# A chunked recurrent layer on one NeuronCore: the state's product as three passes of split parts

## The reference

```python
xn = layernorm(x)
proj = einsum('bld,pd->blp', xn, in_proj_w)      # gate, hbc (x, B, C) and dt
xBC = silu(causal_conv4(hbc))                    # x: 64 heads x 64; B, C: 8 groups x 128
dt = softplus(dt + dt_bias); dA = exp(-exp(A_log) * dt)
# per token t, head h:  state = state * dA + (dt * x) outer B;   y = state @ C
y = y + x * D
yn = y * rsqrt(mean_over_group(y * y) + eps) * norm_weight * silu(gate)
s = einsum('bli,di->bld', yn, out_proj_w)
out = x + s * silu(xn @ W.T + bias + lora)
```

## Time and profile before

| | |
|---|---|
| three runs | 1748.84, 1750.83, 1754.08 us, median 1750.83 |
| the profiled execution | 1753.88 us, of which the span is 1752.1 |
| mean granted TensorE clock | 0.991 of full speed |
| PE / PEld busy | 97% / 78% of the span |
| DVE / POOL / ACT busy | 81% / 68% / 63% |
| DMA | 304.78 MB, mean 174 GB/s |
| chain that ended last, by engine | PE 80%, DMA 5%, DVE 5%, SP's queue 4%, ACT 2%, POOL 2% |

### The profile page before, as it was taken

One profiled execution on the slowest core, in us unless ns is written; L12 is line 12 of the kernel. 1 busy time (PEld: TensorE's weight loads), 2 busy tenths in 40 slices (PEclk: granted clock), 3 DMA queues, 4 the chain that ended last, 5 costly groups with the idle time before them and its releaser, 6 DMA issues.

```text
span 1752.1 us, 31626 instructions
## 1 busy us (share of the span) xinstructions
PE 1697.6 (97%) x10792; PEld 1368.7 (78%) x10792; DVE 1420.8 (81%) x1840; ACT 1098.3 (63%) x2843; POOL 1190.4 (68%) x1255
## 2 busy tenths in 40 slices
PE   7988999999999999999998999999999999999986
PEld 5777888888888888888876888888888888888865
DVE  7868888887978888887876978888887878888885
ACT  4557576665757576665656667575666657576653
POOL 5428677675857767675786858678575857767564
PEclk9999999999999999999999999999999999999998
DMA  8545555555555555555787655565555565555555
GB/s 267 157 134 171 171 176 153 169 173 173 166 177 159 164 169 164 179 173 157 232 227 230 184 174 161 166 180 154 169 174 174 154 184 160 165 166 177 159 166 151
DMA packets 322416, 304.78 MB, mean 174 GB/s; under 512 B 88272, under 2 KB 255568, under 8 KB 322256
## 3 DMA queue, kind: packets, MB, share of 16 engines
q1 hardware_dynamic: 321216, 302.60, 58.0%
q10 hardware_dynamic: 1040, 0.16, 0.1%
HBM read 246.57 MB, written 56.10 MB: 173 GB/s over the span
## 4 chain that ended last, share of the span: by engine, by line
PE 80%; DMA 5%; DVE 5%; SPq 4%; issue 3%; ACT 2%; POOL 2%; ACTq 0%; POOLq 0%; DVEq 0%
PE ps_conv L1381 9%; PE ps_conv L1384 9%; PE ps_y L1544 7%; PE ps_conv L1387 6%; PE ps_out L1381 6%; PE ps_gate L1381 6%; PE ps_s L1565 6%; PE ps_out L1384 6%; PE ps_gate L1384 6%; PE ps_y L1549 5%; PE ps_out L1387 4%; PE ps_gate L1387 4%; DMA turned_d<-squares 3%; PE ps_conv L1388 2%; PE ps_g L1373 2%
## 5 line engine op out<-in xcount | busy, mean ns | idle before, releaser
L930 DVE SCALAR_TENSOR_TENSOR xc<-ps_conv,convw_sb,xc 128x511 f32<-128x511 f32 (+2 forms) x576 | 430.4, 747 | 96.7 <-ACT xc L694 83.1
L1288 POOL TENSOR_TENSOR cpre<-cpre,xc 128x1024 f32<-128x1024 f32 x112 | 268.5, 2397 | 52.8 <-ACT xc L700 29.9
L826 ACT ACTIVATE dtx<-x_tok,prefix_dt 128x64 f32<-128x64 f32 x1024 | 258.1, 339 | 72.1 <-DMA b_tok<-turned_d 72.0
L1321 POOL TENSOR_TENSOR square<-square 128x256 f32<-128x256 f32 x128 | 93.8, 733 | 305.6 <-ACT square L838 305.6
L1070 DVE TENSOR_TENSOR_SCAN decay<-decay,turned_x 128x512 f32<-128x512 f32 x250 | 290.4, 1203 | 9.2 <-DMA decay<-decays_d 9.0
L1381 PE MATMUL ps_conv<-xn_hi,wconv_hi 128*128 128x512 f32 x768 | 245.4, 441 | 0.0
L1384 PE MATMUL ps_conv<-xn_hi,wconv_lo 128*128 128x512 f32 x768 | 206.4, 390 | 0.0
L1381 PEld LDWEIGHTS ps_conv<-xn_hi,wconv_hi 128*128 128x128 f32 x768 | 144.4, 188 | 68.2 <-issue 43.6
L1544 PE MATMUL ps_y<-decay,dtx 128*64 128x128 f32 x1984 | 191.6, 280 | 2.7 <-ACT ps_y L808 2.7
L854 ACT ACTIVATE ynt_hi<-ps_y 128x512 fp32r<-128x512 f32 x126 | 75.2, 597 | 178.2 <-DVE ps_y L1128 175.1
L1549 PE MATMUL ps_y<-cpre,state 128*64 128x128 f32 x1760 | 172.1, 274 | 0.0
(11 more groups left out here) (236 smaller groups left out, 3783.0 us busy)
## 6 DMA issues: line engine op xcount, KB each, us to landing
decay<-decays_d SPq DMA_DIRECT2D x125, 512.0 KB, 5.1
cpre<-rows_d SPq DMA_DIRECT2D x112, 512.0 KB, 4.1
turned_d<-squares SPq DMA_DIRECT2D x512, 80.0 KB, 2.7
stage<-w_in_t SPq DMA_DIRECT2D x32, 1024.0 KB, 6.3
x_tok<-turned_d SPq DMA_DIRECT2D x128, 256.0 KB, 3.0
stage<-w_out_t SPq DMA_DIRECT2D x16, 1024.0 KB, 6.3
stage<-w_in_t SPq DMA_DIRECT2D x32, 256.0 KB, 3.9
b_tok<-turned_d SPq DMA_DIRECT2D x128, 64.0 KB, 2.9
```

Of the source, the lines that this page charges most:

```text
L826: scaled = e.activation(dtx[i % 2][:, h * HD:(h + 1) * HD].rearrange("p (a i) -> p a i", i=SQ), head_of(x_tok[i % 2], h), ACT.Copy, scale= ...
L930: e.scalar_tensor_tensor(acc[:, d:], ps[:, 0:BLK - d], convw_sb[:, tile, TAPS - 1 - d:TAPS - d], acc[:, d:], ALU.mult, ALU.add).then_inc(S ...
L1288: e.tensor_tensor(cpre[k % 2][:, :, :], cpre[k % 2][:, :, :], xc[i // CPB % 2][:, XT + 1, block_cols(i % NCH)].unsqueeze(1).to_broadcast([ ...
```

## The change

The product of L1565 is no longer one native fp32 matmul. `b_tok` and `xw` are each split, as the weights are: ACT makes `b_hi` (128 x 128) and `xw_hi` (128 x 512) by copies to fp32r, at the head of its step before the `dtx` scalings, and POOL makes `b_lo` and `xw_lo` by subtraction at the very head of its step, before `left_of_state`. PE runs the three passes b_hi by xw_hi, b_lo by xw_hi, b_hi by xw_lo. The four new tiles have one buffer each. In the diff below, the first `e.activation` lines are ACT's, `split_state` and `scale_x` are POOL's, and the last hunk is PE's. `scale_x` waits for `xw_lo` of the step before, on its own queue.

```diff
+        xw_hi = sb("xw_hi", [P, GC], F32R)
+        xw_lo = sb("xw_lo", [P, GC], F32R)
+        b_hi = sb("b_hi", [P, NS], F32R)
+        b_lo = sb("b_lo", [P, NS], F32R)
...
                 if 0 <= m < N and conv_late(m) is not None:
                     conv(conv_late(m))
+                if 0 <= m < N and m % NCH < NCH - 1:
+                    w.wait_ge(landed_tok[m % 2], 32 * (m // 2 + 1))
+                    w.wait_ge(S["mm_u"], inner(m) - 1)
+                    e.activation(b_hi[:, :], b_tok[m % 2][:, :], ACT.Copy).then_inc(S["b_hi"], 1)
+                    w.wait_ge(S["xw"], inner(m))
+                    e.activation(xw_hi[:, :], xw[:, :], ACT.Copy).then_inc(S["xw_hi"], 1)
...
+            def split_state(m):
+                w.wait_ge(S["b_hi"], inner(m))
+                w.wait_ge(S["mm_u"], inner(m) - 1)
+                e.tensor_tensor(b_lo[:, :], b_tok[m % 2][:, :], b_hi[:, :].bitcast(F32), ALU.subtract).then_inc(S["b_lo"], 1)
+                w.wait_ge(S["xw_hi"], inner(m))
+                e.tensor_tensor(xw_lo[:, :], xw[:, :], xw_hi[:, :].bitcast(F32), ALU.subtract).then_inc(S["xw_lo"], 1)
...
             def scale_x(i):
-                w.wait_ge(S["mm_u"], inner(i) - 1)
+                w.wait_ge(S["xw_lo"], inner(i) - 1)
...
                 m, u = i - 1, i - DRAIN
                 f = finished(i)
+                if 0 <= m < N and m % NCH < NCH - 1:
+                    split_state(m)
                 if i < N and i % NCH > 0:
                     left_of_state(i)
...
-                    w.wait_ge(landed_tok[m % 2], 32 * (m // 2 + 1))
-                    w.wait_ge(S["xw"], inner(m))
+                    w.wait_ge(S["b_hi"], inner(m))
+                    w.wait_ge(S["xw_hi"], inner(m))
                     w.wait_ge(S["state"], inner(m - 1) if m > 0 else 0)
-                    e.matmul(ps_s[:, :], b_tok[m % 2][:, :], xw[:, :], start=True, stop=True).then_inc(S["mm_u"], 1)
+                    passes(ps_s[:, :], (lambda t: b_hi[:, :], lambda t: b_lo[:, :]),
+                           (lambda t: xw_hi[:, :], lambda t: xw_lo[:, :]), 1,
+                           lambda: w.wait_ge(S["b_lo"], inner(m)), lambda: w.wait_ge(S["xw_lo"], inner(m)), S["mm_u"])
```

More of the change, by code:

```diff
@@ L244, in build @@
             landed_rows0 landed_rows1 st_rows10 st_rows11 st_rows00 st_rows01
-            turned st_turned landed_tok0 landed_tok1 dtx scan last xw mm_g M skip cpre mm_gate sgate mm_in mm_u
+            turned st_turned landed_tok0 landed_tok1 dtx scan last xw b_hi xw_hi b_lo xw_lo mm_g M skip cpre mm_gate sgate mm_in mm_u
             seed state sdec square sum1 sum2 mm_ssq var2 rstd2 yg hi2 lo2 mm_out osum
```

## The result

| | before | after |
|---|---|---|
| median of 7 runs each, us | 1752.9 (1748.8 to 1754.1) | 1758.2 (1756.7 to 1760.2) |
| the profiled execution, us | 1753.88, span 1752.1 | 1757.41, span 1755.4 |
| ratio after / before | | 1.0035, 95% interval 1.0023 to 1.0046 |

The change makes the kernel 0.35% slower. 1744 and a faster kernel were forecast (the change from the profiled execution of before was to be -6.8 us; it is +3.5, and +5.3 between the medians).

The account below looks back on a forecast made before the run. PE was taken to bound 14 of 16 groups. Terms -17.5 (PE), +4.2 (third pass), +5.0 (last group), +1.5 (batch's turn) gave -6.8 us: 1747.1 for the profiled execution, 1744.0 for a median; range 1736 to 1760.

Parts of the forecast that it names:

- The product's price on PE: On PE, native product 0.86 us against 0.68 for three passes: 0.18 saved per product, 17.5 us over 97.
- Rival 3: On PE, three passes into one bank cost as much as the native product, no saving: 1761 us; chance 0.06.
- The four durations: Added operations on POOL and ACT: xw_lo 1.30 us, b_lo 0.46, xw_hi 0.62, b_hi 0.30.
- Third pass at position 1: PE wants xw_lo at 432.07, it ends at 432.1, PE starts at 432.3: a stall of 0.2 to 0.3 us.
- At position 2: PE's third pass: xw_lo at 446.15, wanted at 446.22, just in time; a stall of 0.05 to 0.1 us.
- Position 4: PE's third pass: xw_lo at 470.6, wanted at 471.8, a slack of 1.0 us and so no stall.
- I cost it at nothing: Work behind POOL's split_state: cpre, rstd2 and out_sum come late, out_sum some 1.6 us, but DVE's slack covers it: 0 us.
- The copies "in an idle time of 2.09 before dtx": On ACT at position 1, b_hi and xw_hi run to 430.8 in 2.09 us of idle time, so dtx isn't late.
- First batch's last group and what follows: POOL delays the batch's turn by 1.5 us, bounds 0 and 5; PE's stalls there fall into its later waits.
- Last group: split_state comes ahead of cpre on POOL's chain, two to four times: 5.0 us slower, bounds 0 and 9.
- The second: Rival: PE waits for xw_lo in a POOL, ACT, POOL, PE loop, about 0.5 us per stalled product: 1764 us; chance 0.17.
- The first: Rival: POOL 0.5 us later at positions 2 to 5, PE stalls 0.8 to 1.0 us per group: 1752 us; chance 0.25.

Follow-up runs that it names:

- experiment 1: The change without POOL's two subtractions, PE using the hi parts in all three passes: 1735.7 us, ratio 0.9912 to the kernel before.
- Experiment 8: The change cut to one pass of rounded values, xw written as fp32r by POOL, no low parts, not the same computation: 1689.9 us, ratio 0.9651.
- Experiments 7: The change with ACT's copies b_hi and xw_hi moved ahead of the late tile's tap: 1746.2 us, ratio 0.9963 to the kernel before.
- 10: The change with POOL's cpre ahead of the subtractions at position 3 alone: 1751.7 us, ratio 1.0002 to the kernel before.
- experiment 12: The change with ACT's copies ahead of the tap and the native product wherever fin_multiply and fin_add precede POOL's subtractions: 1737.1 us, ratio 0.9911.
- 2: The change with the native product back in each batch's last group and for step 64's product: 1750.7 us, ratio 1.0002 to the kernel before.
- 9: The change with ACT's copies ahead of the late tap and the native product in groups 7 and 15: 1738.2 us, ratio 0.9932.
- experiment 5: The change with PE reading only hi parts and not waiting for low parts, which POOL still makes: 1757.3 us, ratio 1.0031 to the kernel before.

## Why the prediction was wrong, by its steps

Forecast against measured, both from the profiled executions (12 ordinary groups: 12 x 0.96 = 11.5 of the 97 products' gain less the stalls; group 0: steps 2 to 7). With the first product of both batches left out the forecast should have counted 14 x 7 - 2 = 96 products, a slip of 0.2 us.

| | forecast | measured |
|---|---|---|
| 12 ordinary groups | -11.5 | -4.1 |
| group 0 | -1.0 | +0.6 |
| group 7 | +1.5 | +2.8 |
| group 8 | -0.8 | +2.4 |
| group 15 | +5.0 | +2.7 |
| ahead of group 0's step 2, behind group 15 | 0 | -1.2 |
| sum | -6.8 | +3.3 (the span's) |

- **The product's price on PE: right.** 0.86 less 0.68 was to be 0.18; it is 0.19 (11.43 to 11.24), and experiment 1 gives it seven times per group. Rival 3 is out. Experiment 8 is the check of 0.2275 per pass.
- **The four durations: right** (1.28, 0.46, 0.63, 0.31 against 1.30, 0.46, 0.62, 0.30).
- **Third pass at position 1: right** (0.23). **At position 2 the size came right by luck** (0.10). The rows were those of group 3, where xw ended 1.56 us ahead of PE's sum of squares; in nine of the twelve ordinary groups of before it was 3.0 to 3.2. After, it is 1.41 in all but one.
- **Position 4: the failed step.** It read "a slack of 1.0" from ACT's timeline of before, with b_hi 2.7 ahead of PE's product (468.5 and 471.23). After, b_hi is 1.4 ahead (468.17 and 469.57), and the slack is gone. Measured from PE's sum of squares at position 3 or 4, out_sum came 2.2 us later than before, the taps behind it 1.7, and ACT's silu and b_hi 1.3. Position 6, which had "more", stalls by 0.16 in the same way.
- **What made it fail is the next step, "I cost it at nothing".** It had cpre 2 us late at positions 2 and 4 and out_sum 1.6. Against PE's step cpre is 3.8 and 3.2 late there in the median, and out_sum 2.8 and 3.1. It closed with DVE's mean slack and the 4 to 6 us until PE wants the output. The path that counts doesn't end at the output: it goes rstd2, out_sum, early taps, ACT's silu, b_hi, b_lo, xw_lo, and so back into the edit itself one position on. Experiments 7 and 10 break it in two places, and each time the stall at 4 is gone.
- **The copies "in an idle time of 2.09 before dtx"** were walked for ACT and not for POOL. The copies stand behind a tap that waits for PE, so POOL's head waits with them, 153 us in all. That cpre was ready in this time is shown for position 3 (experiment 10), not for the others; at position 4 it itself waited for ACT in the kernel before. The placement costs 12 us (experiment 7).
- **First batch's last group and what follows: too small.** +1.5 was for the turn, and stalls behind fin_add were to "fall into its own later waits"; and the two steps of group 8 whose blocks are finished had no term. There PE's product shows

```profile
948.30 0.47 PE L1401 MATMUL ps_s<-xw_hi,b_hi 128*128 128x512 f32 x1 [3.03 <-ACT xw_hi L826]
949.27 0.51 PE L1404 MATMUL ps_s<-xw_hi,b_lo 128*128 128x512 f32 x1 [0.50 <-POOL b_lo L1306]
950.49 0.79 PE L1408 MATMUL ps_s<-xw_lo,b_hi 128*128 128x512 f32 x1 [0.72 <-POOL xw_lo L1308]
951.09 1.91 PE L1401 MATMUL ps_conv<-xn_hi,wconv_hi 128*128 128x512 f32 x4
```

  and experiment 12 brings both groups back by leaving the split out there.
- **Last group: the mechanism is right, 2.7 us instead of 5.0.** xw_lo is on the chain three times, and cpre goes after it each time. Where these subtractions were left out, this group took 93.27, 95.11 and 93.57 (experiments 1, 2, 9) and not before's 96.01. Against these the change loses 3.6 to 5.5, so the price of the subtractions may have been sized well; why the group is shorter there than in the kernel before isn't known. Two pieces of the chain, which answer to the first row:

```profile
1667.32 1.28 POOL xw_lo L1308
1668.61 1.62 POOL cpre L1298
```

- **The rivals.** The second, given 0.17, is nearest: slower, by a loop round POOL and ACT. Its place was wrong: it had PE's wait for xw_lo as the price, and experiment 5 takes that wait away and gains 0.9 us, within the noise; its loop passes through DVE. The first (the third pass eats the gain, 0.8 to 1.0 us per group) has the size for ordinary groups (0.9) and the wrong cause.
- last went from 584 ns to 1378: its 110 instances take 87 us more, where the prediction had worked out 8 for them. In the ordinary groups most of that is no cost: at position 3 out_sum would have waited for rstd2 anyway. At position 5 it costs 0.16 us of PE in eight groups. The Trainium skill, SBUF — State Buffer, section Who interferes with whom, has a DVE operation with two SBUF inputs and a GpSimd operation that reads SBUF exclude each other for a whole instruction. The trace agrees: last ends with a POOL instruction, at 460.64 beside cpre's 460.61.

## What to carry to other kernels

An edit that saves on the bounding engine and puts work at the head of another engine's step has to be walked twice round: once for the added instructions, and once for everything behind them until the chain comes back to the edit's own inputs. Measure each time from a fixed point in the bounding engine's step. Read the rows of more than one repetition, since one group can be untypical. Look at what the head instruction waits for: a wait at the head of an in-order queue also holds what is ready behind it, and moving its producer (ACT's copies ahead of a tap that waits for PE) was worth 12 us here. Where a group isn't bound by the engine that saves, leave the edit out there.

## What the hardware showed that I had not expected

- Taking PE's wait away (experiment 5) moved the stall to two other waits and changed an ordinary group by less than 0.1 us.
- A DVE operation of 128x16 was held for 3.75 us, through three POOL instructions in a row (cpre, skip, square), in eight of twelve groups. In the other four it was held for 2.0 to 2.2 and ended with cpre.
- PE's clock dropped twice instead of once at the start of the second batch. Before, the granted clock is 0.57 and 0.50 in 939 to 945, behind 4.08 us of waiting, and 1.00 at 951 to 957. After, it is back at 0.86 in 942 to 945, and falls once more behind the product's waits of 3.03, 0.50 and 0.72 us:

```profile
945.00:951.00 6.00, 1.75 (x11) 1.05 (x8) 3.46 (x5) 3.98 (x13) 4.74 (x5) 0.89 0.58 122
951.00:957.00 6.00, 6.00 (x16) 4.65 (x15) 3.56 (x6) 5.04 (x15) 6.00 (x6) 0.54 0.92 316
```

  The columns are those of the earlier trace rows; 0.50 is the level of 1.2 GHz, 1.00 that of 2.4. The twelve passes behind the product take 5.11 us (951.09 to the next block's start at 956.20) instead of 12 x 0.2275 = 2.73. So the stall costs 2.4 us more there than its own length. The first drop gives 0.9 of it back: the twelve passes of its output block take 4.54 us (939.35 to 943.89) instead of 5.42 in the kernel before (940.58 to 946.00).
